# Batch 1 of the first projection moved between the first maxima of an attention kernel

## What is computed

```
x = x + attn_a(layernorm(x))      # 32 heads of 8, biases, softmax(q k / sqrt(8)) v, Wo
x = x + ffn(layernorm(x))         # silu(x Wg) * (x Wu), the 2 largest of each 4 kept, then Wd
x = x + attn_b(layernorm(x))      # 32 query heads, 8 key heads, a band masked out
x = x + ffn(layernorm(x))
```

## Time and profile before

| | us |
|---|---|
| median of 3 runs | 1861.56 (1858.26 to 1862.22) |
| profiled execution | 1860.73 |
| its span (first to last instruction) | 1859.0 |
| TensorE busy | 1712.1 (92%) |
| VectorE busy | 1496.1 (80%) |
| ScalarE busy | 1280.5 (69%) |
| GpSimd busy | 270.3 (15%) |

### The profile page before, as it was taken

The page is one execution under the profiler, slowest core; times in us unless marked ns, Lnnn a source line. Parts: engine busy times, 40 slices in busy tenths (PEclk is TensorE's granted clock), DMA queues, the critical chain, the costliest instruction groups (busy, mean ns, idle before and its releaser), DMA issues.

```text
span 1859.0 us, 39169 instructions
## 1 busy us (share of the span) xinstructions
PE 1712.1 (92%) x13872; PEld 665.9 (36%) x13872; DVE 1496.1 (80%) x2150; ACT 1280.5 (69%) x2414; POOL 270.3 (15%) x613
## 2 busy tenths in 40 slices
PE   5679999999999999899876999999999999998998
PEld 3312222222222223577552222222222222345766
DVE  6599999999899982565548999999999999526644
ACT  3249999999899996222221899999999999952210
POOL 5000000000000000000011232233322333210000
PEclk9769999999999999999986899999999999989999
DMA  6933354333533321100035132223322231220000
GB/s 223 262 53 63 56 88 72 62 57 68 84 70 62 57 63 37 45 1 0 34 52 149 38 72 46 51 46 68 60 51 52 45 72 38 59 63 1 12 12 23
DMA packets 71996, 114.67 MB, mean 62 GB/s; under 512 B 12336, under 2 KB 27696, under 8 KB 71856
## 3 DMA queue, kind: packets, MB, share of 16 engines
q1 hardware_dynamic: 71856, 112.63, 27.7%
HBM read 71.96 MB, written 40.63 MB: 61 GB/s over the span
## 4 chain that ended last, share of the span: by engine, by line
PE 47%; DVE 39%; issue 10%; DMA 2%; ACT 1%; DVEq 1%; SPq 0%; POOLq 0%; ACTq 0%
DVE mneg L901 21%; PE psum L543 12%; PE psum L605 11%; DVE xn L907 10%; PE psum L525 9%; PE psum L499 5%; PE psum L623 4%; PE psum L470 2%; PE psum L583 1%; DVE mneg L907 1%; PE psum L455 1%; DVE area L945 1%; DVE area L961 1%; PE psum L485 1%; DMA k_stacks<-area 1%
## 5 line engine op out<-in xcount | busy, mean ns | idle before, releaser
L727 ACT ACTIVATE area<-psum 128x512 f32<-128x512 f32 x2048 | 1108.9, 598 | 110.8 <-PE psum L525 87.9
L499 PE MATMUL psum<-area 64*128 64x512 bf16 x2048 | 591.5, 397 | 56.2 <-DVE mneg L907 28.9
L543 PE MATMUL psum<-area 128*32 128x256 f32 x8192 | 641.1, 391 | 0.8 <-POOL area L1084 0.4
L525 PE MATMUL psum<-area 64*128 64x512 bf16 x2048 | 637.3, 385 | 4.4 <-DMA area<-max_rows 3.6
L907 DVE CUSTOM_DVE_ANT_0 xn<-psum,band 128x1024 f32<-128x1024 f32 x512 | 591.1, 1220 | 21.6 <-PE psum L499 21.4
L901 DVE TENSOR_REDUCE mneg<-psum 128x1 f32<-128x1024 f32 x512 | 585.2, 1217 | 20.0 <-PE psum L499 19.9
L543 PEld LDWEIGHTS psum<-area 128*32 128x32 f32 x8192 | 168.8, 108 | 383.2 <-issue 243.5
L525 PEld LDWEIGHTS psum<-area 64*128 64x128 bf16 x2048 | 136.9, 94 | 456.2 <-ACT area L727 408.8
L937 DVE TENSOR_TENSOR area<-psum,area 128x512 f32<-128x512 f32 x64 | 43.7, 691 | 150.0 <-PE psum L605 137.0
L768 ACT ACTIVATE area<-psum 128x512 f32<-128x512 f32 x64 | 38.2, 597 | 182.6 <-PE psum L605 182.5
L605 PE MATMUL psum<-xnT,wg 128*128 128x512 f32 x256 | 133.2, 646 | 27.9 <-DVE area L937 23.6
(11 more groups left out here) (67 smaller groups left out, 748.5 us busy)
## 6 DMA issues: line engine op xcount, KB each, us to landing
ctx_rows<-area SPq DMA_DIRECT2D x64, 256.0 KB, 2.1
area<-q_stacks SPq DMA_DIRECT2D x32, 384.0 KB, 7.8
area<-k_stacks SPq DMA_DIRECT2D x64, 192.0 KB, 6.7
area<-q_stacks_b SPq DMA_DIRECT2D x32, 384.0 KB, 6.1
area<-q_stacks SPq DMA_DIRECT2D x32, 192.0 KB, 4.1
area<-q_stacks_b SPq DMA_DIRECT2D x32, 192.0 KB, 3.3
area<-ctx_rows SPq DMA_DIRECT2D x16, 256.0 KB, 4.6
area<-inv_rows SPq DMA_DIRECT2D x16, 256.0 KB, 5.7
```

The costliest lines, as they stand in the source:

```text
L499: mm = pe.matmul(psum[:, 2 + 2 * (c % 2) + half, :], q_max[lo:lo + PAR, buf, head, tile * P:(tile + 1) * P], k_max[lo:lo + PAR, buf, 0 if ...
L525: pe.matmul(psum[:, S_BANKS[slot % len(S_BANKS)], :], k_st[lo:lo + PAR, buf, 0 if a else head // 2, kt * P:(kt + 1) * P], q_st[lo:lo + PAR ...
L543: mm = pe.matmul(psum[head * VW:(head + 1) * VW, PV_BANK, cols], vaug[:, buf, kt, head, :], probs[:, u % PRING, head, cols], start=(kt == ...
L727: act.activation(probs[:, u % PRING, head, :], psum[:, S_BANKS[slot_of(u, head, ahead) % len(S_BANKS)], :], ACT.Exp, scale=SCALE).then_inc ...
```

## The change

- VectorE makes three clears of 4096 columns at its start (the third is the one that GpSimd made after all stores). GpSimd keeps only the clear of `vaug` (2048 columns), and makes `band` behind its addition to x. The semaphore `area_set` becomes `const_step`, `cleared` and `vaug_set`.
- `parts` has six slots: four at the start of `area` under `probs`, used by both batches of the first attention, and two where they were, which with two of the four serve the second attention as before. `resid` has a buffer for each attention.
- x of batch 1 is loaded behind Wq and Wk.
- TensorE transposes batch 0, projects its q and k, transposes batch 1 and then projects V of batch 0. Batch 1's halves run ahead of the maxima's chunks 0, 2, ... 14, in banks 0 and 1 in turn; its four chunks of V ahead of chunks 9, 11, 13 and 15, in banks 6 and 7.
- VectorE makes the split steps of batch 1 after maxima 0, 2, ... 16, and the additions of V after maxima 10, 12, 14 and 16. ScalarE splits batch 0 before it copies the transposed batch 1.
- The first turned maxima (before chunk 19) wait for all residues and all of V.
- SyncE loads the maxima's stack of group 0 behind the first two quarters, that of group 1 behind all quarters of batch 0, and the score stack of group 0 right after it (in the first attention). It waits for all stores after the first `move_max`.

```diff
-        parts_low, _ = carve(0, [2, PARTS, SEQ], BF16)
-        parts, at = carve(q_st_at, [2, PARTS, SEQ], BF16)
-        parts = [parts[:, 0], parts[:, 1], parts_low[:, 0], parts_low[:, 1]]
-        resid, at = carve(at, [2, BANK], F32)
+        parts_low, at = carve(0, [4, PARTS, SEQ], BF16)
+        resid_low, at = carve(at, [2, BANK], F32)
+        assert at <= ones_at
+        parts_high, at = carve(q_st_at, [2, PARTS, SEQ], BF16)
+        parts = [parts_low[:, i] for i in range(4)] + [parts_high[:, i] for i in range(2)]
+        resid_high, at = carve(at, [2, BANK], F32)
         assert at <= q_max_at
+        resid = [resid_low, resid_high]
...
+        V_BANKS = [[(4, 5), (6, 7)], [(4, 4), (5, 5)]]
+        MAX_CLEARED, ST_CLEARED = (2, 5), (3, 6)
+
+        def proj_bank(a, b, i):
+
+            return i % 2 if a == 0 and b == 1 else (PBASE[a] + b * PCH[a] + i) % 4
...
+        V_CHUNKS = (9, 11, 13, 15)
+
+
+        SLOT = [0, 1, 2, 3, 0, 1, 2, 3] + [4, 5, 4, 0, 1, 5]
...
-            for b in range(BATCH):
-                sp.dma_start(x[:, b * BT:(b + 1) * BT, :],
-                             x_in[b].rearrange("(t p) d -> p t d", p=P)).then_inc(x_loaded[b], 16)
-            for w, src in zip(wqkvo, (wq_a, wk_a, wv_a, wo_a)):
+            sp.dma_start(x[:, 0:BT, :], x_in[0].rearrange("(t p) d -> p t d", p=P)).then_inc(x_loaded[0], 16)
+            for w, src in zip(wqkvo, (wq_a, wk_a)):
+                sp.dma_start(w[:], src.rearrange("(k p) n -> p k n", p=P)).then_inc(w_loaded[0], 16)
+            sp.dma_start(x[:, BT:TILES, :], x_in[1].rearrange("(t p) d -> p t d", p=P)).then_inc(x_loaded[1], 16)
+            for w, src in zip(wqkvo[2:], (wv_a, wo_a)):
                 sp.dma_start(w[:], src.rearrange("(k p) n -> p k n", p=P)).then_inc(w_loaded[0], 16)
...
-                        sp.wait_ge(area_set, 5 + 2 * a)
+                        sp.wait_ge(cleared, MAX_CLEARED[a])
                         load_max_stack(a, 0, 0)
-                        load_max_stack(a, 1, 1)
+                if b == 0:
+                    load_max_stack(a, 1, 1)
...
                 store_stacks(a, 0)
+                if a == 0:
+                    sp.wait_ge(cleared, ST_CLEARED[a])
+                    load_st_stack(a, 0, 0)
                 store_stacks(a, 1)
-                for i in range(4):
-                    sp.wait_ge(stacks_stored[i], stored(i, QBASE[a] + BATCH * NQ[a]))
-                sp.wait_ge(area_set, 6 + 2 * a)
-                load_st_stack(a, 0, 0)
+                if a == 1:
+                    all_stored(a)
+                    sp.wait_ge(cleared, ST_CLEARED[a])
+                    load_st_stack(a, 0, 0)
                 move_max(a, 0, 0, 0)
+                if a == 0:
+                    all_stored(a)
...
+            def project_half(a, b, i):
+                j, half = divmod(i, HALF)
+                w, m, rows = QUARTERS[a][j]
+                n = PBASE[a] + b * PCH[a] + i
+                if i == 0:
+                    pe.wait_ge(w_loaded[a], 64)
+                    pe.wait_ge(ln_evac, 4 * (4 * a + b) + 4)
+                    if a == 1:
+                        pe.wait_ge(hid_done, 28 + 4 * b)
+                behind = 2 if a == 0 and b == 1 else 4
+                if n >= behind:
+                    pe.wait_ge(rest_done, n - behind + 1)
+                for k in range(DK):
+                    mm = pe.matmul(psum[0:rows, proj_bank(a, b, i), :], w_a[a][w][:, k, m * P:m * P + rows],
+                                   xnT[:, k, b * SEQ + half * BANK:b * SEQ + (half + 1) * BANK],
+                                   start=(k == 0), stop=(k == DK - 1))
+                mm.then_inc(proj_ready, 1)
+
+            def project_v(a, b, v):
                 if a == 1:
                     pe.wait_ge(x_fed, 6 + 2 * b)
                 width = (D, KV_HEADS * HD)[a]
                 per = BANK // width
+                n = VBASE[a] + b * VCH[a] + v
+                if n >= 2:
+                    pe.wait_ge(v_done, n - 1)
+                for t in range(per):
+                    tok = b * SEQ + (v * per + t) * P
+                    for k in range(DK):
+                        mm = pe.matmul(psum[:, V_BANKS[a][b][v % 2], t * width:(t + 1) * width], xnT[:, k, tok:tok + P],
+                                       w_a[a][2][:, k, :], start=(k == 0), stop=(k == DK - 1))
+                mm.then_inc(v_ready, 1)
+
+            def project(a, b):
+                for i in range(PCH[a]):
+                    project_half(a, b, i)
                 for v in range(VCH[a]):
-                    n = VBASE[a] + b * VCH[a] + v
...
-                pe.wait_ge(rest_done, PBASE[a] + BATCH * PCH[a])
-                pe.wait_ge(v_done, VBASE[a] + BATCH * VCH[a])
+                pe.wait_ge(rest_done, PBASE[a] + (BATCH, 1)[a == 0] * PCH[a])
+                pe.wait_ge(v_done, VBASE[a] + (BATCH, 1)[a == 0] * VCH[a])
                 for c in range(CHUNKS):
+                    if a == 0 and c < CPH and c % 2 == 0:
+                        project_half(a, 1, c // 2)
+                    if a == 0 and c in V_CHUNKS:
+                        project_v(a, 1, V_CHUNKS.index(c))
                     if c == CPH + 3:
+                        pe.wait_ge(rest_done, PBASE[a] + BATCH * PCH[a])
+                        pe.wait_ge(v_done, VBASE[a] + BATCH * VCH[a])
                         turn_max(a, 0, 0)
                     max_scores(a, 0, 0, c)
...
-            for b in range(BATCH):
-                norm_transpose(0, b)
-            for b in range(BATCH):
-                project(0, b)
+            norm_transpose(0, 0)
+            for i in range(PCH[0]):
+                project_half(0, 0, i)
+            norm_transpose(0, 1)
+            for v in range(VCH[0]):
+                project_v(0, 0, v)
...
-            for b in range(BATCH):
-                norm(0, b)
-                copy_transposed(0, b)
+            norm(0, 0)
+            copy_transposed(0, 0)
+            norm(0, 1)
             act.wait_ge(bias_loaded, 64)
-            for b in range(BATCH):
-                split(0, b)
+            split(0, 0)
+            copy_transposed(0, 1)
+            split(0, 1)
...
                 for c in range(CHUNKS):
                     maxima(a, 0, c)
+                    if a == 0 and c <= CPH and c % 2 == 0:
+                        split_step(a, 1, c // 2)
+                    if a == 0 and c - 1 in V_CHUNKS:
+                        copy_v(a, 1, V_CHUNKS.index(c - 1))
...
+            dve.memset(area[:, q_max_at:q_max_end], 0.0).then_inc(cleared, 1)
+            dve.memset(area[:, ones_at:vaug_at], TWO_ONES[0]).then_inc(cleared, 1)
+            dve.memset(area[:, q_st_at:q_max_at], 0.0).then_inc(cleared, 1)
             for b in range(BATCH):
                 norm(0, b)
             dve.wait_ge(bias_loaded, 64)
-            for b in range(BATCH):
-                split(0, b)
+            split(0, 0)
...
+            def make_band():
+                pool.memset(band[:], MASK).then_inc(const_step, 1)
+                pool.wait_ge(const_step, 2)
+                pool.affine_select(out=band[:], in_=band[:], compare_op=ALU.is_ge, fill=0.0, base=WINDOW - BAND_AT,
+                                   pattern=[[1, 15 * P]], channel_multiplier=-1).then_inc(const_step, 1)
+                pool.wait_ge(const_step, 3)
+                pool.affine_select(out=band[:], in_=band[:], compare_op=ALU.is_gt, fill=0.0, base=BAND_AT,
+                                   pattern=[[-1, 15 * P]], channel_multiplier=1).then_inc(const_step, 1)
+
             for a in range(2):
-
                 if a == 1:
                     pool.wait_ge(o_ready, 8)
-                pool.memset(area[:, q_max_at:q_max_end], 0.0)
-                if a == 1:
+                    pool.memset(area[:, q_max_at:q_max_end], 0.0).then_inc(cleared, 1)
                     pool.wait_ge(down_ready, 8)
-                pool.memset(area[:, ones_at:vaug_at], TWO_ONES[a]).then_inc(area_set, 1)
-                pool.memset(area[:, vaug_at:q_st_at], 1.0)
-                if a == 0:
-
+                    pool.memset(area[:, ones_at:vaug_at], TWO_ONES[a]).then_inc(cleared, 1)
+                pool.memset(area[:, vaug_at:q_st_at], 1.0).then_inc(vaug_set, 1)
+                if a == 0:
                     pool.wait_ge(bias_loaded, 64)
                     pool.wait_ge(ln_xn, BATCH * BT)
                     pool.tensor_tensor(x[:], x[:], bo_rows[:].rearrange("p (o d) -> p o d", o=1).to_broadcast(
                         (P, TILES, D)), ALU.add).then_inc(x_biased, 1)
-                for i in range(4):
-                    pool.wait_ge(stacks_stored[i], stored(i, QBASE[a] + BATCH * NQ[a]))
-                pool.memset(area[:, q_st_at:q_max_at], 0.0).then_inc(area_set, 1)
+                    make_band()
+                else:
+                    for i in range(6):
+                        if stored(i, QBASE[a] + BATCH * NQ[a]):
```

(54 more changed lines are left out.)

88 lines of the change are left out of this document (21 added, 67 removed).

## The result

The changed kernel took 1852.95 us (median of 7 runs, 1848.39 to 1854.13) against 1860.78 for the kernel before (7 runs). The ratio is 0.9955, with a 95% interval of 0.9944 to 0.9967: 8 us faster, where 9.2 were forecast. The profiled execution has a span of 1851.2 us against 1859.0, 7.8 less.

A forecast was written before the change was run, and what follows sets the result against it. TensorE and VectorE were taken to share the last-ending chain. First maximum 23.6 us earlier, 32 maxima 50.6 us instead of 36.0: gain 9.2, so 1851.5 from the profiled execution, 1852.4 from the median; given 1852, range 1845 to 1860.

The forecast's parts named there:

- Clears: Kernel start: three VectorE clears of 4096 columns, 4.3 us each, begun at about 0.8, done at 13.7 us.
- (a): Kernel start: fast memsets move everything up to the maxima by up to 6.3 us; gain 15.5, 1846.9; chance 0.11.
- Start and blocked subtraction: First xn at 17.7, projection from 22.9; VectorE's first subtraction stands behind GpSimd's addition until 36.0, ending 36.6, 1.9 us later.
- Band: GpSimd's band, 5.3 us beside batch 0's subtractions, delays them by 2 us, bounds 0 to 5.3.
- Split of batch 0: Ends at 48.5 us instead of 44.2, with TensorE's last two halves at 3.4 us each after its clock falls.
- First maximum: First attention: starts at 60.7 us instead of 84.33, 23.6 earlier; projection, not the loads, is the later path.
- 32 maxima: Leading maxima with batch 1 interleaved: 50.6 us instead of 36.0, including 14.3 of added VectorE work and 0.3 of waits.
- (b): Interleaved maxima: a pair at half clock and late bank exchanges lose 3 to 5 us; 1856; chance 0.14.
- (c): Maxima 0 to 15: TensorE stays at half clock throughout, 19 us more, 1871, sign turned; chance 0.07.
- Turned maxima: Before chunk 19: ScalarE waits for batch 1's last store, landed by 100; ready at 106, TensorE wants them about 109.
- The sum: Whole kernel: maxima end at 111.3 instead of 120.5, each later stage 9 us earlier; gain 9.2 us.
- the store wait: Ahead of V: TensorE's 16.13 us wait for a store of stacks behind loads, taken out by the change.

The follow-up runs named there:

- late addition: GpSimd's addition to x and the band moved behind the first split of maxima, against the changed kernel; 1841.73 us, ratio 0.9905 to the kernel before.
- fourth clear: One more VectorE clear of 4096 columns at the start, against the changed kernel; 1856.27 us, ratio 0.9986 to the kernel before.

## Why the prediction was right

**Clears: right.** 13.7 forecast, 13.68 measured, from two shapes of another instruction. The steps are 4.27 us as forecast (4.3), but the rows start at 1.75 and not at 0.8, and the statistics start 3.39 behind the third clear and not 4.27; the two cancel. The rival of fast clears (a) is out.

**Start and blocked subtraction: right.** First xn at 17.61 (17.7), projection at 23.06 (22.9), GpSimd's addition until 36.08 (36.0), the blocked subtraction until 36.64 (36.6). The late addition showed that this block is the cause and not a companion.

**Band: 2 taken, 1.48 measured**, two subtractions that lost 0.74 each beside a selection, none for the memset. That is chance in part: with a fourth clear the same selections cost 1.63 and 0.74, because VectorE met them at another moment. The rule of the Trainium skill, "SBUF — State Buffer", section "Who interferes with whom", bounded it rightly, at no more than the selections.

**Split of batch 0: 48.5 forecast, 47.6 measured.** The clock fell later than I placed it, at about 47.4 (mean 0.92 from 44 to 48 us), so the last two halves ran fast (3.70 us for both) and V began slow. Stores landed 5.3 us behind the issue (42.49 to 47.78), not 7.0; they were not the later path.

**First maximum: 60.7 forecast, 60.24 measured. 32 maxima: 50.6 forecast, 50.3 measured.** The second agreement is two errors that cancel. VectorE's added work was 12.5 us and not 14.3: between two maxima a split step takes 1.26 us from start to start (64.30 to 65.56) and an addition of V 0.60 (84.39 to 84.99), less than the 1.45 and 0.68 of the rows. The waits cost 1.6 us, not 0.3: 0.16 and 0.27 (twice) of idle time ahead of maxima 10, 12 and 14, 0.57 ahead of maximum 19, and a little more for the overlap that each breaks. The 0.57 is GpSimd's added wait for all of V, which I had at nothing: GpSimd began its copy of V at 93.09, and TensorE could turn the first maxima only at 95.00. Rival (b) had this mechanism, at 3 to 5 us; its half clock did not come, nor did (c): the clock stayed at 1.00 through the interleaved part and fell behind it.

**Turned maxima: covered.** ScalarE copied them at 97.85 (I had 100), TensorE first used them at 108.85.

**The sum: 9.2 forecast; 10.0 at maximum 32, 7.8 in span, 8 in the medians.** The term that is missing is TensorE's clock at the later pauses, 2.1 us here (9.78 - 7.67), which I had at nothing ("each later stage is 9 us earlier"). Its size is chance: the second execution of the same kernel had a span 5.9 us shorter.

**What I told wrong** is the account, not the time. I priced the moved loads only for the second attention, at nothing, named the store wait as taken out by the new arrangement, and did not ask how much of it the moved loads alone would take out. In the old kernel they alone give the whole 9 us. (The 16.13 us, too, are the store's way from issue to landing; ScalarE's waits for slots were 10.93 and 1.44.) The rest of the change comes out near nothing on top of that: VectorE's clears (-3.3) and the band behind the addition (-1.3) pay back what the interleaving brings (4 to 5). This balance is added up from runs that each moved one part; no single run shows it. Once GpSimd's work is moved out of the way, slots, order and interleaving are worth 0.9923 - 0.9875 = 0.0048, 9 us.

What stays open: whether a particular pause of TensorE costs 3.4 or 6.8 us of half clock could not be told from the work around it. It differed between executions of the same kernel. Open, too, is how much the moved loads matter inside the changed kernel, where batch 1's slots are needed later.

## What to carry to other kernels

Before a stage is rebuilt around a wait, ask what is queued ahead of the transfer that ends it: eight loads stood before stores that batch 1 needed, and moving only the four that belong to the next group gave the gain. Price an instruction that moves to another engine by what it delays there, and look whether the engine that it leaves was idle. GpSimd's instructions that read SBUF did least harm here where VectorE reads PSUM, beside the maxima.

## What the hardware showed

- A VectorE clear of 4096 float32 columns has a record of 3.47 us, but the next starts 4.27 us behind it, and with one more clear the statistics are 4.27 later: the time between starts is 1.04 ns a column, the record is not the cost. Only behind the last clear does the next row start earlier, by 3.39 us, so the rows of clears probably start some 0.9 us late (a reading of these rows, not tested). The Trainium skill, "VectorE: DVE Perf Modes", section "Zero memsets can be issued as uint32 (trn2)", has one cycle for each element; the starts agree, the records don't.
- GpSimd's clears (3.51 us, write only) hold VectorE's one-input normalisation of SBUF data (5.76 us for eight in place of 2.68) but not its two-input subtraction (0.68). GpSimd's addition holds the subtraction to its very end (6.57), and a selection does the same: the held subtraction ended 0.54 to 0.56 us behind the end of GpSimd's instruction in each case, whether it had lost 0.74, 1.63 or 5.89 us.
- TensorE's first half of the first projection took 3.9 us in the changed kernel (23.06 to ScalarE's first copy of it at 26.91) and 2.5 in the kernel before (26.89 to 29.36), where the first half of batch 1 took 2.0 (48.45 to 50.43), while the granted clock reads 1.00 in all of them.
- Executions of one kernel differ in how long TensorE stays at half clock behind the same pauses, and by up to 6 us in time (1848.39 to 1854.13): 54.5 and 41.8 us between copies 31 and 32 in two executions of the changed kernel.
